# A four-layer Perceiver kernel: expert activations shared between ScalarE and GpSimd, self-attention by head group, an expert gather in bf16 parts

## The reference

```python
# L1A: self-attention, 16 heads of 128 channels
qkv = xn @ w_qkv;  P = softmax(q @ k.T / sqrt(128))
out = (P weighted v) @ w_o

# L2F: 8 experts of 2048 for each of 8 heads and each token
z   = act(dot(h, down_embed[index]) * softmax(score))      # act(z) = z * sigmoid(z) = z / (1 + exp(-z))
out = sum over 8 heads x 8 experts of z * up_embed[index]

# L3X: linear attention on the context; k' = relu(k Wkf), kv = k'.T v, out = (q' kv) / (q' sum k')

# L3F: 64 experts, 6 per token, each expert takes its tokens up to a capacity
buf = x[tokens of the expert]; out = (silu(buf @ w_gate) * (buf @ w_up)) @ w_down, summed back by weight
```

## Time and profile before

| | |
|---|---|
| median of 3 runs | 1235.15 us (1233.06 to 1237.44) |
| the profiled execution | 1236.14 us |
| its span | 1234.2 us |
| PE busy | 1088.1 us, 88% |
| PE weight loads | 760.5 us, 62% |
| DVE busy | 683.6 us, 55% |
| ACT busy | 484.1 us, 39% |
| POOL busy | 195.2 us, 16% |
| mean granted clock of PE | 0.944 of full speed |

### The profile page before, as it was taken

The page is one execution under the profiler, slowest core; times in us unless marked ns, Lnnn a source line. Parts: engine busy times, 40 slices in busy tenths (PEclk is TensorE's granted clock), DMA queues, the critical chain, the costliest instruction groups (busy, mean ns, idle before and its releaser), DMA issues.

```text
span 1234.2 us, 22895 instructions
## 1 busy us (share of the span) xinstructions
PE 1088.1 (88%) x9353; PEld 760.5 (62%) x9353; DVE 683.6 (55%) x1524; ACT 484.1 (39%) x1080; POOL 195.2 (16%) x190
## 2 busy tenths in 40 slices
PE   6988899995976999999999998988699984887998
PEld 5866666664754555555555666775465553776886
DVE  3544357772343667766566642647457786545332
ACT  1111147771320335555555674533244441141222
POOL 0002200000000000000000000004786788110000
PEclk9998999996997999999999999999699997887999
DMA  9012300004001200000000002012444444005551
GB/s 382 14 59 95 120 1 2 2 2 164 3 1 48 116 1 2 2 2 2 2 1 2 2 2 83 2 59 80 135 124 138 132 128 121 15 1 213 214 213 52
DMA packets 16182, 84.38 MB, mean 68 GB/s; under 512 B 3152, under 2 KB 3664, under 8 KB 12368
## 3 DMA queue, kind: packets, MB, share of 16 engines
q1 hardware_dynamic: 7888, 57.75, 12.3%
q0 software_dynamic: 8192, 25.17, 7.1%
HBM read 82.65 MB, written 0.26 MB: 67 GB/s over the span
## 4 chain that ended last, share of the span: by engine, by line
PE 68%; POOL 12%; DVE 10%; issue 5%; ACT 3%; DMA 1%; POOLq 0%; SPq 0%; DVEq 0%; ACTq 0%
POOL L2F_rows L2521 9%; PE L2X_bank_ring L1778 7%; PE L2X_bank_ring L1794 6%; PE L2X_bank_read L1808 6%; PE L2X_bank_ring L1717 4%; PE L1X_banks_scores L916 3%; PE L2X_bank_ring L1726 2%; PE L0X_bank_k L457 2%; PE L3F_bank_y L3390 2%; PE L0X_bank_moments L468 2%; PE L3F_bank_gathered L3339 2%; PE L3F_bank_gate_up L3350 2%; PE L1X_bank_proj L893 2%; PE L1A_bank_qk L1181 2%; POOL L2F_z_exp L2503 2%
## 5 line engine op out<-in xcount | busy, mean ns | idle before, releaser
L2077 DVE TENSOR_REDUCE L2X_max_parts<-L2X_bank_ring 128x1 f32<-128x512 f32 x256 | 158.3, 683 | 85.7 <-PE L2X_bank_ring L1778 85.6
L1988 ACT ACTIVATE L2X_context_exp<-L2X_bank_ring 128x384 f32<-128x384 f32 (+1 forms) x384 | 144.1, 464 | 62.5 <-PE L2X_bank_ring L1794 59.6
L2521 POOL DMA_INDIRECT L2F_rows<-in_L2F_embed_dram,L2F_expert x128 | 132.1, 1032 | 60.9 <-issue 36.6
L1778 PE MATMUL L2X_bank_ring<-L2X_context_kT,L2X_q_masked 32*128 32x512 f32 x512 | 96.9, 630 | 0.0
L1024 ACT ACTIVATE L1X_probs<-L1X_clipped,L1X_drop,L1X_keep 128x1024 f32<-128x1024 f32 x64 | 77.6, 1237 | 30.7 <-DVE L1X_clipped L1084 23.5
L1084 DVE TENSOR_SCALAR L1X_clipped<-L1X_banks_scores 128x1024 f32<-128x1024 f32 x64 | 75.4, 1219 | 24.6 <-PE L1X_banks_scores L916 22.9
L1794 PE MATMUL L2X_bank_ring<-L2X_q_and_max,L2X_context_kT 32*128 32x384 f32 (+1 forms) x768 | 85.9, 497 | 0.0
L1808 PEld LDWEIGHTS L2X_bank_read<-L2X_context_exp,L2X_context_v_ones 128*32 128x32 f32 x2048 | 50.2, 109 | 43.8 <-issue 33.4
L1808 PE MATMUL L2X_bank_read<-L2X_context_exp,L2X_context_v_ones 128*32 128x128 f32 x2048 | 75.8, 277 | 1.1 <-ACT L2X_context_exp L1988 0.8
L2752 DVE SCALAR_TENSOR_TENSOR x<-L2F_rows,L2F_expert_weight,x 128x256 f32<-128x256 f32 x128 | 62.4, 487 | 4.6
L2623 ACT ACTIVATE L3X_k_features<-L2F_banks_pair 128x1024 f32<-128x1024 f32 x32 | 32.8, 1024 | 66.7 <-remote 51.9
(11 more groups left out here) (627 smaller groups left out, 2047.4 us busy)
## 6 DMA issues: line engine op xcount, KB each, us to landing
L3F_expert_weights<-in_L3F_experts_dram SPq DMA_DIRECT2D x16, 1280.0 KB, 5.6
L1A_groups<-in_L1A_groups_dram SPq DMA_DIRECT2D x3, 1536.0 KB, 9.6
ctxT<-in_ctxT_dram SPq DMA_DIRECT2D x8, 512.0 KB, 11.1
L0X_tokens<-in_L0X_tokens_dram SPq DMA_DIRECT2D x8, 512.0 KB, 15.0
slot<-in_L1A_dram SPq DMA_DIRECT2D x1, 3584.0 KB, 11.5
slot<-in_L0F_dram SPq DMA_DIRECT2D x1, 3072.0 KB, 10.3
slot<-in_L2A_dram SPq DMA_DIRECT2D x1, 3072.0 KB, 10.5
slot<-in_L2F_dram SPq DMA_DIRECT2D x1, 2476.5 KB, 9.0
```

The source lines that it names most:

```text
L1778: nc.tensor.matmul(bank[:, :], qm[32 * g:32 * g + 32, b, c, j, :], cT[32 * g:32 * g + 32, s % 3, blk * 512:(blk + 1) * 512], start=True, s ...
L1988: nc.scalar.activation(ex[:, n % NE, g, 0:width(s)], bank_of(s_e, done(n) + g + 1)[:, 0:width(s)], ACT.Exp, scale=SCALE).then_inc(s_e, 1)
L2077: nc.vector.tensor_reduce(parts[:, j, g, blk:blk + 1], bank_of(s_ft, n)[:, :], AX, ALU.max).then_inc(s_ft, 1)
L2521: pool.indirect_dma_start(out=rows[:, r, k, :], out_offset=None, in_=env.dram["L2F_embed"], in_offset=bass.IndirectOffsetOnAxis(idx[:, b, ...
```

## The change

Three sublayers are edited.

In L1A, v of two heads is projected right after q and k of the same two heads. The column sums use two banks in turn and wait for the values of the unit two before. The products with `w_o` are split by unit (`out_part`) and stand one group behind the scores; only the last group's are left for the end. 14 idle products stand in front of the turn of `xn`.

In L2F, six of the exponentials (pieces 11 to 16) are made by ACT, after its loop of 32 steps and after the first four parts of `finish(0, ...)`. Five more (pieces 1, 3, 5, 7, 9) are made by ACT at the end of steps 6, 11, 16, 23 and 30. The other six stay on POOL. `finish(0, ...)` moves behind the loop on PE and ACT, the two softmax exponentials move to steps 19 and 28, and the idle products become 18.

In L3F, the normalised tokens are split into three bf16 parts that add up to the fp32 value, by four operations on DVE. `in_seat` is bf16. One gather is 12 products in bf16 instead of 4 in fp32.

```diff
-    bank_v, bank_c = L.bank("v"), L.bank("colsum")
+    bank_v, bank_c = L.bank("v"), (L.bank("colsum"), bank_x)
...
-            for j in range(HG // 2):
-                n = g * (HG // 2) + j
-                if n >= 1:
-                    pe.wait_ge(s_vc, n)
-                for h in range(2):
-                    for k in range(KC):
-                        i = nc.tensor.matmul(bank_v[:, h * T:(h + 1) * T], wt(g, 2, 2 * j + h, k), head.xT[:, k, :],
-                                             start=(k == 0), stop=(k == KC - 1))
-                i.then_inc(s_v, 1)
+                if h % 2:
+                    project_values(g, h // 2)
+
+        def project_values(g, j):
+            n = g * (HG // 2) + j
+            if n >= 1:
+                pe.wait_ge(s_vc, n)
+            for h in range(2):
+                for k in range(KC):
+                    i = nc.tensor.matmul(bank_v[:, h * T:(h + 1) * T], wt(g, 2, 2 * j + h, k), head.xT[:, k, :],
+                                         start=(k == 0), stop=(k == KC - 1))
+            i.then_inc(s_v, 1)
...
-            if u:
-                pe.wait_ge(s_val, u)
-
-            nc.tensor.matmul(bank_c[:, :], env.const("ones"), pn[:, u % 2, :, :].rearrange("p h t -> p (h t)"),
+            if u >= 2:
+                pe.wait_ge(s_val, u - 1)
+            nc.tensor.matmul(bank_c[u % 2][:, :], env.const("ones"), pn[:, u % 2, :, :].rearrange("p h t -> p (h t)"),
                              start=True, stop=True).then_inc(s_c, 1)
 
+        def out_part(u):
+            g, b = units[u]
+            pe.wait_ge(s_val, u + 1)
+            for h in range(g * HG, (g + 1) * HG):
+                i = nc.tensor.matmul(bank_o[:, b * D:(b + 1) * D], val[:, h, b * P:(b + 1) * P], w("w_o")[:, h * D:(h + 1) * D],
+                                     start=(h == 0 and b == 0), stop=(h == 15), skip_group_check=True)
+            if u == len(units) - 1:
+                i.then_inc(s_out, 1)
+
         env.wait_weights(pe, "L1A")
-        head.tensor(pe)
+        head.tensor(pe, 14)
         pe.wait_ge(head.s_xT, 1)
         project_group(0)
         for g in range(NG):
             for b in range(B):
                 scores(g * B + b)
+            if g:
+                for b in range(B):
+                    out_part((g - 1) * B + b)
             if g + 1 < NG:
                 project_group(g + 1)
             for b in range(B):
                 column_sums(g * B + b)
-        pe.wait_ge(s_val, len(units))
         for b in range(B):
-            for h in range(16):
-                i = nc.tensor.matmul(bank_o[:, b * D:(b + 1) * D], val[:, h, b * P:(b + 1) * P], w("w_o")[:, h * D:(h + 1) * D],
-                                     start=(h == 0), stop=(h == 15))
-        i.then_inc(s_out, 1)
+            out_part((NG - 1) * B + b)
...
-    exp_behind = {(m + 2, TOP // 2 - 1): m for m in range(last - 2)}
-    exp_behind.update({(last - 1, TOP - 1): last - 2, (last, TOP - 3): last - 1})
+    LATE = 11
+    exp_step = {6: 1, 11: 3, 16: 5, 23: 7, 30: 9}
+    exp_behind = {(m + 2, TOP // 2 - 1): m for m in range(LATE) if m not in exp_step.values()}
+
+    def on_scalar(m):
+        return m >= LATE or m in exp_step.values()
...
-    FRONT, FINISH = 2, 26
+    FRONT = 2
...
-            if n == FINISH:
-                pe.wait_ge(s_kc, 2 * (len(steps) // 4))
             if n == NT + 4:
                 turn_kv(0)
-            if n - FINISH < 5:
-                finish(0, n - FINISH, bank_k, bank_k, (bank_k, bank_k), bank_k)
         summary(len(steps) - 1)
+        pe.wait_ge(s_kc, 2 * (len(steps) // 4))
         pe.wait_ge(s_fc, len(steps))
+        for n in range(5):
+            finish(0, n, bank_k, bank_k, (bank_p0, bank_p1), bank_k)
         pe.wait_ge(s_z, len(pieces))
-        idle_products(M, bank_v, 24)
+        idle_products(M, bank_v, 18)
...
-        for m in range(last, len(pieces)):
-            exp_z(m)
...
+        def exp_z(m):
+            _, lo, hi = pieces[m]
+            act.wait_ge(s_z, m + 1)
+            nc.scalar.activation(ze[:, m % 3, lo:hi], zz[:, m % 3, lo:hi], ACT.Exp, scale=-1.0).then_inc(s_ze1, 1)
...
-            if n in (17, 23):
-                part = 2 if n == 17 else 3
+            if n in exp_step:
+                exp_z(exp_step[n])
+            if n in (19, 28):
+                part = 2 if n == 19 else 3
...
-                finish(0, n - FINISH, bank_k, bank_k, (bank_k, bank_k))
         copy_kv(1)
+        for n in range(4):
+            finish(0, n, bank_k, bank_k, (bank_p0, bank_p1))
+        for m in range(LATE, len(pieces)):
+            exp_z(m)
...
-            dve.wait_ge(s_ze, m + 1)
+            dve.wait_ge(s_ze1 if on_scalar(m) else s_ze, sum(on_scalar(k) == on_scalar(m) for k in range(m + 1)))
...
-    here = L.sb("in_seat", [P, NB, B, PER * CAP])
+    here = L.sb("in_seat", [P, NB, B, PER * CAP], BF16)
+    NPART = 3
+    part, rest = L.sb("xn_parts", [P, NPART, B, D], BF16), L.sb("xn_rest", [P, B, D])
...
-                for b in range(B):
-                    i = nc.tensor.matmul(bank_ga[:, k * PER * CAP:(k + 1) * PER * CAP], head.xn[:, b, k * P:(k + 1) * P],
-                                         here[:, j % NB, b, :], start=(b == 0), stop=(b == B - 1))
+                for m in range(NPART):
+                    for b in range(B):
+                        i = nc.tensor.matmul(bank_ga[:, k * PER * CAP:(k + 1) * PER * CAP], part[:, m, b, k * P:(k + 1) * P],
+                                             here[:, j % NB, b, :], start=(m == 0 and b == 0), stop=(m == NPART - 1 and b == B - 1))
...
+        pe.wait_ge(s_parts, 1)
         gather(0)
...
+        dve.wait_ge(head.s_norm, B)
+        chain(nc.vector.tensor_copy(part[:, 0, :, :], head.xn[:, :, :]))
+        chain(nc.vector.tensor_tensor(rest[:, :, :], head.xn[:, :, :], part[:, 0, :, :], ALU.subtract))
+        chain(nc.vector.tensor_copy(part[:, 1, :, :], rest[:, :, :]))
+        nc.vector.tensor_tensor(part[:, 2, :, :], rest[:, :, :], part[:, 1, :, :], ALU.subtract).then_inc(s_parts, 1)
```

More of the change, by code:

```diff
@@ L1294, in scale_values @@
             nc.vector.tensor_tensor(val[:, g * HG:(g + 1) * HG, b * P:(b + 1) * P], vT[:, g % 2, :, b * P:(b + 1) * P],
-                                    bank_c[:, :].rearrange("p (h t) -> p h t", h=HG), ALU.mult).then_inc(s_val, 1)
+                                    bank_c[u % 2][:, :].rearrange("p (h t) -> p h t", h=HG), ALU.mult).then_inc(s_val, 1)
         copy_values(0)
@@ L2220, in layer_L2F @@
              "q_done", "q_copied", "sim_done", "sim_copied", "shifted", "softmax_exp", "experts_ready", "z_ready", "z_exp_ready",
-             "rows_used", "h_ready", "base_set")
+             "rows_used", "h_ready", "base_set", "z_exp_by_scalar")
     (s_chain, s_up, s_pre0, s_pre1, s_ue, s_h1, s_h, s_hT, s_hn, s_q, s_qc, s_sim, s_simc, s_sh, s_se, s_idx, s_z, s_ze,
-     s_used, s_hnc, s_base) = (L.sem(n) for n in names)
+     s_used, s_hnc, s_base, s_ze1) = (L.sem(n) for n in names)
     s_rows = [L.sem(f"rows_gathered{r}") for r in range(NR)]
@@ L3305, in layer_L3F @@
              "gathered", "gathered_copied", "gate_up_done", "tanh_ready", "silu_ready", "hidden_ready", "hidden_turned",
-             "hiddenT_ready", "share_turned", "shareT_ready", "down_done", "rows_copied", "shared_added", "job_added")
+             "hiddenT_ready", "share_turned", "shareT_ready", "down_done", "rows_copied", "shared_added", "job_added", "xn_split")
     (s_chain, s_r, s_re, s_sel, s_rank, s_clear, s_here, s_share, s_ga, s_xg, s_gu, s_e, s_a, s_h, s_t, s_hT, s_st, s_sT, s_o, s_eo,
-     s_ys, s_y) = (L.sem(n) for n in names)
+     s_ys, s_y, s_parts) = (L.sem(n) for n in names)
     env.prefetch(L, None)
```

## The result

| | before | changed |
|---|---|---|
| median of 4 runs | 1235.13 us | 1201.01 us |
| lowest and highest | 1233.06, 1237.44 | 1199.21, 1204.11 |
| ratio, 95% interval | | 0.9732 (0.9708 to 0.9756) |
| profiled execution's span | 1234.2 us | 1199.6 us |
| chain: PE, DVE, POOL | 68%, 10%, 12% | 71%, 14%, 6% |

It is rival A's: the step of the loop that gives the exponential of piece 1 is in time.

The account below looks back on a forecast made before the run. It read the kernel as bound by a chain of waits, PE 68%, POOL 12%, DVE 10%. 1236.14 - 16.5 (L1A) + 14.7 (L2F with L3X) - 6.0 (L3F) = 1228.3 profiled, so median 1227; range 1203 to 1236.

Parts of the forecast that it names:

- rival A: L2F: step 6 comes in time, so the stretch changes by -9 and the time is 1203 to 1204; chance 22%.
- ACT and PE are at this time far from step 6 ... it is there at 907.6: L2F: piece 1's exponential, behind step 6's value copy on ACT, comes at 907.6; before, it was made by 886.20.
- the price of a microsecond: L2F: each microsecond of step 6 is one microsecond of time above the break-even.
- at 883 to 886: L2F: lower bound for step 6, if ACT and PE lose their early waits; nothing is late, stretch -9.
- the program up to there is the same, and so is POOL's traffic: L2F: reason given against step 6 coming in time, an outcome put at 22%.
- break-even of 892: L2F: time of step 6, about 892, above which each microsecond of lateness costs one of time.
- the term of +21.4: L2F: DVE goes on 21.4 us later, waiting for piece 1's exponential, and the delay is carried to the end.
- Those of 1, 3 and 5 ... the choosing absorbs: L2F: taking exponentials 1, 3 and 5 off POOL gains nothing, as DVE's choosing of experts absorbs it.
- L1A: L1A: the new order removes PE's waits and the cold stretch at the output; -16.5 us, bounds 14 and 18.5.
- L3F: L3F: 12 bf16 products take 1.125 us a gather, 0.375 less; over 16 jobs -6.0 us.
- my bound by DVE's copy: L3F: DVE's copy of expert rows must be ready when y starts; 0.57 us a job to spare, at most -9.1.
- The tail: After the last z: with 18 idle products in place of 24, DVE is the later one; -0.5 us.

Follow-up runs that it names:

- e5: The changed kernel with the exponential of piece 1 at the end of step 10 of ACT's loop in place of step 6: 1220.58 us, ratio 0.9881.
- e6: The changed kernel with the exponentials of pieces 1, 3, 5, 7 and 9 back on POOL: 1206.77 us, ratio 0.9772.
- e10: The changed kernel with two bf16 parts of the normalised tokens in L3F in place of three: 1264.74 us, ratio 1.0211.
- e11: The changed kernel with DVE's copy of the expert rows ahead of the product of silu with up in L3F: 1259.16 us, ratio 1.0164.
- e12: The changed kernel with exponentials of pieces 0 to 10 also on ACT and the expert-row copy ahead of silu times up: 1276.97 us, later 1187.15.
- e9: The changed kernel without the 14 idle products at the start of L1A: 1263.38 us.

## Why the prediction was wrong

- **The step that failed** is "ACT and PE are at this time far from step 6 ... it is there at 907.6". The z's, the queue behind it and the price of a microsecond were right (e5); ACT's exponential, put at 0.2, takes 0.20. The time of step 6 was read from the one trace there was, and that trace was disturbed: ACT stood 51.9 us in waits without a named releaser, PE was busy 0.45 of 5 us between 865 and 870, and its granted clock was 0.50 for the next 20 us. The prediction did name the undisturbed time: step 6 "at 883 to 886" is its lower bound, and rival A had it with 22%, 1203 to 1204. What was wrong is the reason that it gave against A, "the program up to there is the same, and so is POOL's traffic". With the same program and the same traffic, step 6 of the kernel before ends 49.6 us after the first z in one trace and 23.45 in the next. From the first z of the trace that I read, 23.45 us lead to 885.7, ahead of the break-even of 892 that the prediction itself gives. So DVE waited 1.92 us for ACT where before it had waited 2.34 for POOL, and the term of +21.4 was nothing.
- **"Those of 1, 3 and 5 ... the choosing absorbs":** wrong, 1.8 us are saved there (e6). With the step in time the stretch gains about 8.4 us (186.9, 187.6 and 187.7 in the three traces without waits that have the old L2F; 179.2, 179.8 and 178.0 in the three of the changed kernel), and rival A's -9 was close.
- **L1A** -16.5: measured 17.6. Back to back is right; the start was better: the idle products took 4.79 us where I had 5.5, and the first product is at 300.48, not 301.7. In part this is luck: in the trace where they took 5.85, the gain is 16.6.
- **L3F** -6.0: measured 4.6. The gather's price was right (1.10 for 1.125), but my bound by DVE's copy allowed 0.57 a job where 0.28 is all there is (6.19 to 5.91): the wait for the copy stands in front of y's first weight load, 0.19, and not only in front of its first product. Before, that load began at 1144.04, while the gather ran until 1144.37; now it begins at 1112.93, 0.06 after the copy's end. 15 times 0.375 - 0.28 is the missing 1.4 (e10), and e11, where the copy comes earlier, gets 1.3 of it back.
- **The tail** -0.5: about -0.8 in the mean of the traces (60.8 in the four with 24 idle products, 59.9 in the fifteen with 18), while they scatter by up to 3 us. The piece that the edit touches, from the last z to L3X's addition to `x`, took 18.6 to 19.5 us in the four and 18.6 in the fifteen.
- **The fastest version** is e12: 1187.15, ratio 0.9619, in an undisturbed occasion, and the slowest, 1276.97, in the disturbed one.

## What to carry to other kernels

Before a trace's times of a background loop are used as a due time for new work, take a second trace of the same kernel: a loop with slack can be late by 26 us in one execution, and nothing in the kernel's time tells. Waits with no named releaser were the sign of it here. Work put on such a loop takes the loop's slack away, so the time becomes as uncertain as the loop. With five exponentials in the loop this kernel takes 1201 us when nothing disturbs it, and e10 and e11, which have the same five, took some 1260 when something did. With none in the loop it takes 1206.8 (e6) undisturbed; what it takes disturbed was not measured. And where PE waits for another engine's result, the wait stands in front of the weight load of the product, so that load is no longer hidden, even if it reads nothing of that result (y's reads `L3F_shareT`).

## What the runs showed of the hardware

The waits without a named releaser occur only while POOL's indirect gathers run, in five traces, none of which has one in another sublayer. While they last, PE too gets its products slowly, one each 0.72 us in e11 (the first two rows of its timeline here), and waits for nothing shown. From the first z to the last, such idle time of PE adds up to 12.6 us in the first trace of before and to 25.6 to 33.3 in e9 to e12; it is 0.0 in the other fourteen.

```profile
860.83 0.37 PE L2423 MATMUL L2F_bank_sim<-L3X_k_features,L3X_v_ones 128*34 128x128 f32 x1 [1.01 <-issue]
...
861.55 0.43 PE L2423 MATMUL L2F_bank_sim<-L3X_k_features,L3X_v_ones 128*34 128x128 f32 x2 [0.34 <-issue]
...
848.00 0.37 PE L2399 MATMUL L2F_banks_pair<-slot,L3X_kT 64*128 64x256 f32 x1 [0.35 <-issue]
...
868.77 1.02 ACT L2640 ACTIVATE L3X_k_features<-L2F_banks_pair 128x1024 f32<-128x1024 f32 x1 [12.92 <-remote]
```

The last two rows say more of these waits. In e11, PE's record of the features of step 2 ends at 848.37, and ACT starts to copy them at 868.77, 20.4 us later. In the changed kernel's trace ACT starts 0.07 us after PE's record ends (865.34 and 865.41 at step 6). The semaphore that ACT waits for is in the trace too: in e11 it rises at 868.75, 0.02 us before ACT starts. So ACT was waiting for PE, whose signal came 20 us after the record that should give it, and the profile names no releaser because the two lie so far apart. Whether PE's work or only its signal was late, the trace does not tell.

The waits came in the first trace of the kernel before, in all four kernels measured on one occasion, and in none of the other fourteen traces, six of which are from the same chip as those four. What makes them stays open. That PE lacks instructions while gathers fill the queues would fit its slow products, but no run here shows it: the packets that carry instructions in this stretch are as many in e11 as in the changed kernel, 15, and the 16 KB ones took as long on average, 1.1 us.

The bf16 products of 192 columns follow each other every 92 ns with weight loads of 98 ns each beside them.
